# Eight tiles' sums moved from VectorE to ScalarE and GpSimd, two tiles' statistics moved back to VectorE

## The reference, cut to what matters

```python
def _L0_xattn_ref(embeds, patch_embeds, patch_lens, W_in, b_in, g_res, g_init):
    h = rmsnorm(embeds, g_res)
    h = jnp.einsum('bld,ed->ble', h, W_in) + b_in
    h_patch = rmsnorm(patch_embeds, g_init)
    return _hnet_depool(h, h_patch, patch_lens)
...
x = x + _L0_xattn_ref(_layernorm(x, axis=-1), ctx_2048, mask_BxS2_if0, ...)
x = x + _L0_ffn_ref(_layernorm(x, axis=-1), L0_ffn_w1, L0_ffn_b1, L0_ffn_w2, L0_ffn_b2)
```

## Time and profile before

| | us |
|---|---|
| median of 3 runs | 832.13 |
| lowest, highest run | 831.93, 834.19 |
| the profiled execution, its own time | 834.93 |
| its span, first to last instruction | 833.2 |
| TensorE busy in the span | 822.3 |
| VectorE, ScalarE, GpSimd busy | 315.9, 294.0, 258.0 |
| first matmul of the feed-forward groups | 118.20 after the span's start |

### The profile page before, as it was taken

How to read it: one execution, slowest core, us unless ns; L and a number is a source line. 1 busy time by engine, 2 the same in 40 slices (tenths; PEclk the granted TensorE clock), 3 DMA queues, 4 the chain that set the end, 5 groups by cost and what they waited for, 6 DMA issues and landing times.

```text
span 833.2 us, 10703 instructions
## 1 busy us (share of the span) xinstructions
PE 822.3 (99%) x3722; PEld 675.9 (81%) x3722; DVE 315.9 (38%) x513; ACT 294.0 (35%) x542; POOL 258.0 (31%) x238
## 2 busy tenths in 40 slices
PE   7999999999999999999999999999999999999998
PEld 5877878788888888888888888888888888888886
DVE  5899852665141423233332423143113411241112
ACT  5668446422622253224422262222222222222221
POOL 2254659940633035301630062305300250011000
PEclk9999999999999999999999999999999999999999
DMA  9988994260236022602233113302300240010001
GB/s 227 281 263 282 291 301 153 89 163 22 68 102 160 0 76 88 167 7 74 72 113 80 50 58 103 50 0 101 51 1 1 79 72 0 0 50 1 1 0 51
DMA packets 39057, 78.11 MB, mean 94 GB/s; under 512 B 6369, under 2 KB 6369, under 8 KB 37265
## 3 DMA queue, kind: packets, MB, share of 16 engines
q1 hardware_dynamic: 30052, 65.95, 24.3%
q0 software_dynamic: 4608, 8.39, 6.4%
q10 hardware_dynamic: 4368, 3.42, 1.5%
HBM read 51.02 MB, written 22.84 MB: 89 GB/s over the span
## 4 chain that ended last, share of the span: by engine, by line
PE 81%; POOL 7%; DVE 4%; DMA 3%; issue 2%; SPq 1%; ACT 1%; ACTq 0%; POOLq 0%; DVEq 0%
PE acc L889 13%; PE acc L890 13%; PE acc L891 13%; PE h_bank L889 13%; PE h_bank L890 13%; PE h_bank L891 13%; DMA xa_odd<-in_x_dram 2%; POOL w_lo L545 2%; PE t_bank L948 2%; POOL x_cur L651 1%; POOL x_next L577 1%; DMA scan_table<-cl_next 1%; POOL cl L564 1%; POOL w_lo L551 1%; DVE h_lo L1070 1%
## 5 line engine op out<-in xcount | busy, mean ns | idle before, releaser
L1303 DVE TENSOR_TENSOR h_lo<-g_f,h_hi 128x512 fp32r<-128x512 f32 x128 | 101.1, 790 | 432.1 <-ACT g_f L826 432.1
L824 ACT ACTIVATE h_hi<-h_bank,b_c 128x512 fp32r<-128x512 f32 x128 | 87.9, 687 | 429.5 <-PE h_bank L891 425.9
L889 PE MATMUL h_bank<-xt_hi,w_hi 128*128 128x512 f32 x512 | 199.9, 390 | 0.6 <-POOL w_lo L545 0.6
L889 PE MATMUL acc<-w_hi,h_hi 128*128 128x512 f32 x512 | 199.8, 390 | 0.0
L891 PE MATMUL h_bank<-xt_hi,w_lo 128*128 128x512 f32 x512 | 199.3, 389 | 0.0
L890 PE MATMUL h_bank<-xt_lo,w_hi 128*128 128x512 f32 x512 | 199.2, 389 | 0.0
L891 PE MATMUL acc<-w_hi,h_lo 128*128 128x512 f32 x512 | 199.2, 389 | 0.0
L890 PE MATMUL acc<-w_lo,h_hi 128*128 128x512 f32 x512 | 199.2, 389 | 0.0
L889 PEld LDWEIGHTS h_bank<-xt_hi,w_hi 128*128 128x128 f32 x512 | 96.1, 188 | 20.7 <-issue 1.0
L891 PEld LDWEIGHTS h_bank<-xt_hi,w_lo 128*128 128x128 f32 x512 | 96.1, 188 | 20.0
L891 PEld LDWEIGHTS acc<-w_hi,h_lo 128*128 128x128 f32 x512 | 96.1, 188 | 20.0
(11 more groups left out here) (168 smaller groups left out, 701.1 us busy)
## 6 DMA issues: line engine op xcount, KB each, us to landing
out_dram<-x_cur SPq DMA_DIRECT2D x32, 256.0 KB, 2.1
x_next<-x_part SPq DMA_DIRECT2D x7, 1024.0 KB, 5.0
w_raw<-in_L_ffn_w_dram SPq DMA_DIRECT2D x6, 1024.0 KB, 9.0
scan_table<-cl SPq DMA_DIRECT2D x6, 896.0 KB
ch<-in_ctx_dram SPq DMA_DIRECT2D x20, 256.0 KB, 2.9
cl<-in_ctx_dram SPq DMA_DIRECT2D x5, 1024.0 KB
xa_odd<-in_x_dram SPq DMA_DIRECT2D x16, 256.0 KB, 7.3
x_part<-xa_odd SPq DMA_DIRECT2D x16, 256.0 KB, 3.9
```

Source lines behind the costliest of these rows:

```text
L824: act.activation(h_hi[:, m % HB, :], h_bank[m % 2][:], ACT.Gelu, bias=b1_c[:, m:m + 1])
L889: nc.tensor.matmul(dst, a_hi, b_hi, start=first, stop=False)
L1303: dve.tensor_tensor(h_lo[:, m % HB, :], g_f32[:], h_hi[:, m % HB, :].bitcast(F32), ALU.subtract).then_inc(h_split, 1)
```

## The change

The sums of tiles 5, 7, 9, 11, 13, 15, 17 and 19 are made in two steps. ScalarE writes product times scale from PSUM into one of the two rows of `ch` (free at that time), and signals `sums_scaled`; this releases the PSUM bank. GpSimd then adds the row to x in the tile's slot and signals `pool_added`. ScalarE's step for tile t stands in turn t + 1 behind the high half of tile t + 3, GpSimd's at the head of turn t + 1. The statistics of tiles 21 and 23 go from ScalarE (turns 15 and 17) to VectorE (turns 17 and 19). TensorE, SP and GpSimd count the remaining adds of VectorE by their place in `BY_DVE`, and SP's first loads into `ch` wait for all eight sums.

```diff
-ON_ACT = (6, 8, 10, 18, 20, 21, 22, 23, 24, 25, 26, 27)
+ON_ACT = (6, 8, 10, 18, 20, 22, 24, 25, 26, 27)
 ON_DVE = tuple(t for t in range(NT) if t not in ON_ACT)
+BY_POOL = tuple(range(5, 20, 2))
+BY_DVE = tuple(t for t in range(NT) if t not in BY_POOL)
+ND = len(BY_DVE)
...
+        def wait_read(engine, t):
+
+            if t in BY_POOL:
+                engine.wait_ge(sums_scaled, BY_POOL.index(t) + 1)
+            else:
+                engine.wait_ge(acc_read, BY_DVE.index(t) + 1)
...
             def store_x1(t):
                 if t >= TI + SR:
                     wait_apart(sp, x1_stored[t % SR], 16 * ((t - TI) // SR))
-                wait_apart(sp, acc_read, t + 1)
+                if t in BY_POOL:
+                    wait_apart(sp, pool_added, BY_POOL.index(t) + 1)
+                else:
+                    wait_apart(sp, acc_read, BY_DVE.index(t) + 1)
...
                 if t == 22:
+                    wait_apart(sp, pool_added, len(BY_POOL))
                     load_high_half(NA, 0)
...
+            def add_scaled(t):
+                n = BY_POOL.index(t)
+                pool.wait_ge(sums_scaled, n + 1)
+                pool.tensor_tensor(xa(t), xa(t), ch[:, n % 2, :], ALU.add).then_inc(pool_added, 1)
+
             for t in range(NT):
+                if t - 1 in BY_POOL:
+                    add_scaled(t - 1)
...
+            def scale_sums(t):
+
+                n = BY_POOL.index(t)
+                act.wait_ge(h_used, t + 1)
+                act.wait_ge(ra_ready, t + 1)
+                if n >= 2:
+                    act.wait_ge(pool_added, n - 1)
+                u = t % XR
+                act.activation(ch[:, n % 2, :], p_bank[t % 3][:], ACT.Copy, scale=ra[:, u:u + 1]).then_inc(sums_scaled, 1)
...
             for t in range(NT):
                 if 2 <= t < NT - 2:
                     tile_high(t + 2)
+                if t - 1 in BY_POOL:
+                    scale_sums(t - 1)
...
             def project(t):
                 pe.wait_ge(x_lo, t + 1)
                 if t >= 3:
-                    pe.wait_ge(acc_read, t - 2)
+                    wait_read(pe, t - 3)
...
             for t in range(NT):
-                if t > 0:
+                if t > 0 and t - 1 in BY_DVE:
                     tile_add(t - 1)
```

More of the change, by code:

```diff
@@ L319, in xattn_ffn @@
         acc_read = sem("acc_read")
+        sums_scaled = sem("sums_scaled")
+        pool_added = sem("pool_added")
         w_hi_done = sem("w_hi_done")
@@ L488, in group @@
                 for i in range(TI):
-                    wait_apart(sp, acc_read, NT + TI * g + i + 1)
+                    wait_apart(sp, acc_read, ND + TI * g + i + 1)
                     sp.dma_start(out_v[g, :, i, :], x_cur[:, i, :]).then_inc(out_stored, 16)
@@ L990, in _ @@
                 project(t)
-            pe.wait_ge(acc_read, NT - 2)
+            pe.wait_ge(acc_read, ND - 2)
             pe.wait_ge(block_ready, NA)
@@ L1012, in ffn2 @@
                 if m == 0:
-                    pe.wait_ge(acc_read, NT + TI * g)
+                    pe.wait_ge(acc_read, ND + TI * g)
                 if m < 12:
```

## The result

The changed kernel takes 837.1 us (median of 5 runs, 836.78 to 838.58) where the kernel before takes 832.1 (5 runs, 831.58 to 834.19): a ratio of 1.0060, interval 1.0045 to 1.0076. The forecast was 832.0 with a range to 834.7, so the change is slower by nearly twice what the range allowed. The profiled execution takes 837.1 us itself, span 835.4.

A forecast was written before the change was run, and what follows sets the result against it. TensorE, 99% busy, was taken as the bound, with at most 2.01 us of stalls to win. Stalls gained 1.5 us, given back at the count; the gate gave -0.1, so 832.13 became 832.0 us, whole range 829.9 to 834.7.

The forecast's parts named there:

- The stalls before tiles 11 and 13: TensorE's waits for low halves in the first stage: shrink by about 1.2 to 1.7 us, given back at the count.
- The race for the one-hots of turn 14: VectorE's second one-hots against GpSimd's sum of tile 13: VectorE starts first, 1.21 us against 1.24 after the high half's start.
- The slower rival: Turn 14: GpSimd's sum of tile 13 seizes SBUF before the one-hots; 833.1, or 834.4 if hit again; chance 0.22.
- The gate: GpSimd's rc_next holds ScalarE until 64.14, so tile 16's high half, the one-hots and counting wait; worth -0.1 us.
- The statistic of tile 21: Moved to VectorE's queue ahead of block 1, where it costs 0.86 us.
- In the change, these statistics come 1.3 us earlier ... The two cancel: rc_next moves by 0, or -0.1.: GpSimd's chain to rc_next: tile 15's statistics 1.3 us earlier, tile 11's sum adds 1.3, so no net move or -0.1.
- Turn 6 ... I let it eat the 0.66.: GpSimd's sum of tile 5 blocks one more VectorE mask operation by up to 1.3 us, eating tile 5's 0.66 saving.
- The copy in turn 14 delays tile 17's high half by 0.5 ... pay it back at once.: ScalarE: the scaled copy costs 0.5 us, repaid at once by statistics 21 and 23 leaving turns 15 and 17.
- Block 1 "0.4 earlier": VectorE's block 1 of the scan: saves 2 x 0.66 on tiles 15 and 17, pays 0.86 for statistic 21.
- GpSimd's queue ahead of the gathers: Scales, the sum of tile 19 and scales again end near 89.6, 1.8 us before the gathers at 91.4: covered.
- The base: The profiled execution, 834.9 us, taken as 2.8 us above the median of the runs, and that difference subtracted.
- The second gate: Chain from block 1 through gathers to normed rows: TensorE cannot finish the stage earlier; only some 0.1 us of wait.

The follow-up runs named there:

- e7: Kernel before with only the statistics of tiles 21 and 23 moved to VectorE, all sums on VectorE: 833.78 us, ratio 1.0003.
- e17: Changed kernel with GpSimd's sum of tile 11 alone moved behind rc_next in turn 12: 836.09 us, ratio to before 1.0037.
- e13: Changed kernel run again unchanged, on one chip with the kernel before: 837.64 us, ratio 1.0069.
- e14: Kernel before, unchanged, profiled again, found in its faster form: 832.79 us, ratio 1.0010.
- e2: Changed kernel with GpSimd's eight sums left out, ScalarE's copies, waits and moved statistics kept: 833.21 us, ratio to before 1.0003.
- e10: Changed kernel with both GpSimd's sums and ScalarE's scaled copies left out, signals alone remaining: 832.38 us, ratio to before 1.0006.
- e6: Changed kernel with GpSimd's additions of b_in to tiles 2 and 3 moved behind the counts of turn 17: 836.48 us, ratio to before 1.0036.
- e3: Changed kernel with the statistics of tiles 21 and 23 back on ScalarE, all eight sums kept: 836.18 us, ratio to before 1.0035.
- e15: Changed kernel with 24 memsets of 21 columns, reading nothing, in place of each GpSimd sum: 835.60 us, ratio to before 1.0040.
- e1: Kernel before, run again unchanged: 833.02 us, ratio 0.9997.
- e12: Kernel before with GpSimd's add_bias of blocks 1 to 3 moved behind the counts, to turn 19: 831.70 us, ratio 0.9999.
- e11: Changed kernel with only sums 15, 17, 19 on GpSimd, add_bias blocks 2 and 3 behind the counts, statistics 21 and 23 on ScalarE: 834.03 us, ratio to before 1.0024.

## Why the prediction was wrong, point by point

Held:
- The stalls before tiles 11 and 13 vanish, and the count gives them back: 0.38 and 0.35 us of transposes, 2.19 at the count.
- The race for the one-hots of turn 14: VectorE first, by 0.02 us. The slower rival bet on the other outcome and is not what happened, though the size of its range (833.1 to 834.4) was closer.
- The groups are untouched, and SyncE's waits cost nothing.
- The gate: rc_next holds ScalarE, and its chain starts at VectorE's statistic of tile 15.
- The statistic of tile 21 costs block 1 what it was put at: 0.88 us in e7 for 0.86.

Failed:
- **"In the change, these statistics come 1.3 us earlier ... The two cancel: rc_next moves by 0, or -0.1."** This is the step that failed. The sum of tile 11 was sized well (1.26 us for 1.3; e17). Two things were not. First, what the chain itself loses beside VectorE's scans was put at nothing: its small steps took 0.33 + 0.82 us longer, and the whole chain 6.87 us for 4.45. Second, the earlier statistics are earlier only against the slow profile that was read (45.44 before, 43.43 changed, so 2.0 us and not 1.3). Against the faster form they are 0.41 us later (43.07, 43.48 in e13). Measured: rc_next +0.53 us against the profile that was read, +2.93 against e14. An earlier statistic would have brought little in any case. In e2 and e10, without the sums, it comes 0.6 to 0.7 us earlier than in e14, the chain then takes 5.64 us for 4.45, and rc_next is at 48.21 and 48.31 for 48.12. The prediction asked what GpSimd's sum does to VectorE, and priced it for GpSimd itself at 1.3; the sum of tile 9 took 3.03.
- **"Turn 6 ... I let it eat the 0.66."** Too small. In e13 three mask operations are held up for 1.2 us each, in e14 one; tile 9's low half starts 2.7 us later than in e14 (28.4 against 25.7 after the first product). The lighter turns 8 to 12 win nearly all of this back: the statistic of tile 15 is 0.4 us behind, and tile 14's low half, with the add of tile 11 gone from before it, 0.3 us ahead (43.4 against 43.7). That last gain had no taker, since tile 16's low half waits for rc_next: 2.6 us behind (53.1 against 50.5).
- **The scans and counts of turns 16 and 17 were left out.** The text named scans as work "of the kind that suffers", and then costed only the one-hots. The scans took 3.40 us for 2.71, the counts 2.63 for 0.61: +0.7 and +2.0 us. The 0.7 are no price of the sums: e2 and e10 have no sum and scans of 3.41 as well. With the add of tile 15 gone the scans start 0.7 us nearer to what stands before them, and end where they would have. The 2.0 are the second place of the loss. The sum of tile 15 (75.88) pushes two bias products onto the counts, each of which blocks a count of 0.2 us for a product's length. Undoing the push gives back 1.76 us at the counts (e6).
- **"The copy in turn 14 delays tile 17's high half by 0.5 ... pay it back at once."** Not paid back: from rc_next to low half 17 it is 6.07 us in e13 (57.12 - 51.05) and 5.79 in e14, though the one-hots start 0.3 us nearer to rc_next in e13. Without sums the copies cost nothing (e2, e10), so this is a term of 0.28 us, or up to 0.6 with the one-hots' nearer start, only on a path that rc_next has made late; that it is the copy was not tested.
- **Block 1 "0.4 earlier".** 5.43 us later in e13 than in e14: 2.93 up to rc_next, 0.28 to low half 17, 2.03 at the counts, the rest (0.19) the add of 17 less and the statistic of 21 more, 0.86 - 0.67; the scans' 0.7 and the add of tile 15, 0.67, cancel. The groups are 6.06 later, 0.63 more.
- **GpSimd's queue ahead of the gathers: "Covered", with a margin of 1.8 us.** Used up, and some 0.5 of the 0.63 us arise here; the rows stand below this list.
- **The base.** One profiled execution 2.8 us above its runs was taken as if all of it were a constant offset. Part of it was another form of the same kernel, one in which VectorE's statistic, and so GpSimd's chain, is late anyway and the change therefore looks cheap.

GpSimd's first gather in e14, then in e13:

```profile
89.30 1.81 POOL L577 DMA_INDIRECT x_next<-scan_table,idx  x1 [3.72 <-DMA scan_table<-cl_next]
```

```profile
94.81 1.99 POOL L595 DMA_INDIRECT x_next<-scan_table,idx  x1 [0.99 <-POOL idx L586]
```

In e14 GpSimd waits for the stored block; in e13 the gather follows the scales, the sum of tile 19 and the indices in its queue. It starts 5.94 us later where block 1 is 5.43 later, and TensorE waits 0.7 us in turn 31 for the normed rows. The second gate was closed already in the profile that was read. The prediction took its wait from turn 30 (0.1 us), and turn 31 of the same profile has 0.65:

```profile
114.50 1.11 PE L948 MATMUL t_bank<-ident,n_rows 128*128 128x128 f32 x8 [0.65 <-DVE n_rows L1212]
```

Without the two moved statistics this wait is gone (e3), and the groups start 1.56 us earlier than in e13.

The sum by the measured terms: 2.93 + 0.28 + 2.03 + 0.19 + 0.63 = 6.06 us between e14 and e13. The medians of that series differ by 5.9 (837.64 - 831.76), or by 4.9 from the runs of e14 itself (832.79); those of the first by 5.0. The marks compare the change with the faster form, and the runs are of both.

On the lock itself, the trace first: beside GpSimd's memsets, casts of 26 elements waited (0.75 to 1.28 us) and the one-hots, of two operands in SBUF, did not; beside GpSimd's sums and products, both did (the one-hots `oh_q`, 1.42 us beside products in e14, 1.01 in e13 without one). The Trainium skill, page SBUF — State Buffer, section Who interferes with whom, has it so: two SBUF inputs on VectorE contend only with a GpSimd instruction that reads, while a cast or copy in a two-port mode contends with GpSimd whatever it does. No trace here names the mode of a cast. The prediction cited this rule and its worst case, 6.8 us more for VectorE to do; the trace had the places where it would strike.

## What to carry to other kernels

Before moving work to an idle-looking engine, list the chains that the engine feeds, and ask for each what else waits in its queue: GpSimd was 31% busy, and the sum of tile 11, ahead of one four-element scale, still cost its full length on TensorE (e17). Test first what the removal alone is worth, by leaving the work out: here nothing, with the two statistics moved (e2, e10), so no cheaper home for the adds could have won. Where the profile names a releaser, compare its time and the kernel's own waits before building on it: the one named for this chain was not waited for. And look at two or three executions of the kernel before, since a profile of its slower form hides a loss that the faster form will show.

## What the runs showed of the hardware

- A cast waited not for one instruction but for a row of them: 24 memsets of some 0.05 us each, issued back to back, kept a cast of 0.18 us waiting for all 1.28 us (e15).
- Very small operations pay in full: counts of eight elements a partition went from 0.60 to 2.63 us for three, a four-element step on GpSimd from 0.19 to 0.56.
- Which side loses is a matter of the start: a sum of 1.3 us that began at 51.45 took 3.03 beside one-hots begun at 51.44, which kept their 1.88 (e13); the counts, beside products of GpSimd, were the ones that waited.
- The arrival of one 128-row tile 0.6 us later (17.9 against 17.3 after the first product) went with 1.9 us at rc_next in kernels without early sums (e1, e12), by way of one more operation of 0.18 us that was held up for 1.28; in e11 such a hold-up gave 1.0 us with no later load.
